# Last layer of a two-layer transformer kernel: rows of a mixture of experts scattered by choice and summed at the end, against rows added into the result by the scatter itself

## What is computed

```python
logits = jnp.clip(xt @ gate_w.T, -50.0, 50.0)       # xt: 2048 tokens x 512, layer-normed; 8 experts
top_w, top_idx = jax.lax.top_k(logits, 2)
rw = jax.nn.softmax(top_w, axis=-1)
# every expert is one 512 x 512 map: W plus a sparse part of its own
out = xt @ W.T + contrib.T                          # = sum over the 2 choices of rw * (map of expert) @ token
x = x + jnp.tanh(g_ffn[1]) * out
```

## Time and profile before

| | us |
|---|---|
| three runs | 2134.19, 2135.01, 2143.93 |
| median | 2135.01 |
| span of the profiled execution, first to last instruction | 2124.4 |
| median over that span (launch and end lie outside the span) | 10.6 |
| last stage, in the span | 1863.6 to 2124.4 |
| its unit loop, first to last scatter | 1960.7 to 2086.0 |
| from the last scatter to the end | 38.4 |

### The profile page before, as it was taken

How to read it: one execution, slowest core, us unless ns; L and a number is a source line. 1 busy time by engine, 2 the same in 40 slices (tenths; PEclk the granted TensorE clock), 3 DMA queues, 4 the chain that set the end, 5 groups by cost and what they waited for, 6 DMA issues and landing times. The chain is left out here.

```text
span 2124.4 us, 39274 instructions
## 1 busy us (share of the span) xinstructions
PE 1848.2 (87%) x11423; PEld 1398.2 (66%) x11423; DVE 1189.7 (56%) x2716; ACT 941.3 (44%) x2679; POOL 996.6 (47%) x1046
## 2 busy tenths in 40 slices
PE   4588999999987999999999999957799998862992
PEld 1355665666556999999999999954466665421781
DVE  5566777777643875422222353328677778670445
ACT  3367676776751432322222333322667666520110
POOL 1477778787621263243333333322655544153551
PEclk9999999999978999999999999988899999985996
DMA  8578877788725588688988888644444454187647
GB/s 321 182 229 275 261 235 232 244 261 252 235 70 183 127 159 191 201 228 259 297 253 239 258 222 220 133 87 123 104 98 109 104 117 101 41 229 207 199 160 272
DMA packets 218788, 409.75 MB, mean 193 GB/s; under 512 B 50794, under 2 KB 116979, under 8 KB 212244
## 3 DMA queue, kind: packets, MB, share of 16 engines
q1 hardware_dynamic: 159132, 319.40, 49.1%
q0 software_dynamic: 31616, 62.14, 13.3%
q10 hardware_dynamic: 27840, 25.70, 4.9%
HBM read 210.46 MB, written 154.20 MB: 172 GB/s over the span
## 5 line engine op out<-in xcount | busy, mean ns | idle before, releaser
L704 ACT ACTIVATE a_P<-a_SC,a_nm 128x256 f32<-128x256 f32 x512 | 235.5, 472 | 132.4 <-DVE a_nm L606 130.8
L1227 POOL DMA_INDIRECT b_y_rows<-b_ysb,b_entry x79 | 124.6, 1577 | 333.8 <-ACT b_ysb L1378 193.6
L606 DVE TENSOR_REDUCE a_nm<-a_SC 128x2 f32<-128x512 f32 x256 | 164.8, 685 | 140.8 <-PE a_SC L850 140.8
L569 POOL TENSOR_TENSOR a_praw<-a_praw,a_phigh 128x704 f32<-128x704 f32 (+2 forms) x126 | 191.5, 1520 | 10.3
L1479 DVE TENSOR_TENSOR b_xl<-b_XT,b_xh 128x512 fp32r<-128x512 f32 x97 | 67.1, 692 | 214.4 <-ACT b_xh L1384 211.7
L861 PEld LDWEIGHTS a_T<-ident,a_P 128*128 128x128 f32 x1024 | 119.2, 145 | 77.8 <-issue 40.4
L861 PE MATMUL a_T<-ident,a_P 128*128 128x128 f32 x1024 | 147.7, 283 | 24.1 <-DVE a_PT L618 22.3
L567 POOL CAST a_phigh<-a_praw 128x704 fp32r<-128x704 f32 (+2 forms) x126 | 111.9, 888 | 95.4 <-DMA a_praw<-in_L_ffn_wd 37.7
L2205 ACT ACTIVATE c_P<-c_SC,c_nm 128x240 f32<-128x240 f32 x256 | 115.5, 456 | 77.1 <-DVE c_P L2077 77.1
L1378 ACT ACTIVATE b_ysb<-b_Y 128x512 f32<-128x512 f32 x79 | 47.2, 597 | 227.2 <-PE b_Y L1322 226.4
L1485 DVE TENSOR_TENSOR b_al<-b_AT,b_ah 128x384 fp32r<-128x384 f32 x111 | 61.9, 558 | 145.9 <-ACT b_ah L1389 145.6
(11 more groups left out here) (519 smaller groups left out, 4984.3 us busy)
## 6 DMA issues: line engine op xcount, KB each, us to landing
w_parts<-a_phigh SPq DMA_DIRECT2D x72, 352.0 KB, 3.7
w_parts<-a_praw SPq DMA_DIRECT2D x72, 352.0 KB, 3.9
b_wh<-w_parts SPq DMA_DIRECT2D x18, 1216.0 KB, 11.7
b_wl<-w_parts SPq DMA_DIRECT2D x18, 1216.0 KB, 14.9
c_q<-c_qT SPq DMA_DIRECT2D x64, 256.0 KB, 4.1
c_k<-c_kT SPq DMA_DIRECT2D x124, 128.0 KB
b_wh<-w_parts SPq DMA_DIRECT2D x18, 704.0 KB, 5.1
b_wl<-w_parts SPq DMA_DIRECT2D x18, 704.0 KB, 7.3
```

The costliest lines, as they stand in the source:

```text
L569: eng.tensor_tensor(raw[:, 0:k * m], raw[:, 0:k * m], r32(high[:, 0:k * m]), ALU.subtract).then_inc(plow_done, 1)
L606: eng.tensor_reduce(nm[:, g % 4, j, :], SC[j][:, :].rearrange("p (t k) -> p t k", t=BT), AX.X, ALU.max, negate=True).then_inc(topped, 1)
L704: e = eng.activation(Pr[:, i, t, :], SC[j][:, t * S:(t + 1) * S], ACT.Exp, bias=nm[:, g % 4, j, t:t + 1], accum_out=den[:, h, t:t + 1])
L1227: eng.indirect_dma_start(out=y_rows, out_offset=bass.IndirectOffsetOnAxis(ap=entry[:, r, 1:2].bitcast(U32), axis=0), in_=ysb[:, v % RING, ...
```

## The change

The result tensor `out` gets 128 rows more (dropped at the end) and first receives the sums x; each unit's rows are then added into it by the scatter.

- `keep_sums` stores x into `out` for batches 0 to 6 during the attention of layer 1 (before: 0 to 3, into a tensor of their own). The last batch and 128 rows of zeros are stored at the head of the last stage.
- A list entry has two values, not three: the place by choice is gone. Empty places point to the 128 rows past the tokens.
- POOL's `send_rows` becomes `add_rows`. A row of `out` is now touched by two units, of different experts. Scatter r waits until scatter r - 2 has landed, and until all scatters of earlier experts have; so the first unit of each expert waits for the unit just before it. Units of the same expert have no token in common, and two of them may be under way. Unit 2 waits for unit 1 too, since the plan's count is at least one scatter, and each of the units 36 to 38 waits for the one before it, since all share the 128 spare rows.
- The plan gets a third row with these counts, by 9 more small operations on VectorE.
- The loads of both choices, the 32 additions, the stores, and the reloads of x are gone.

```diff
-            def send_rows(r):
+            def add_rows(r):
+                if r:
+                    prior = eng.value_load(plan_i[0:1, 2, r:r + 1], min_val=16, max_val=16 * NR)
+                    eng.wait_ge(y_sent[1 - r % 2], prior)
+                    eng.sem_inc(others_added, 1)
+                ge(eng, y_sent[r % 2], 16 * (r // 2))
                 eng.wait_ge(y_scaled, r + 1)
                 eng.indirect_dma_start(
-                    out=y_rows, out_offset=bass.IndirectOffsetOnAxis(ap=entry[:, r, 2:3].bitcast(U32), axis=0),
-                    in_=ysb[:, r % RING, :], in_offset=None).then_inc(y_sent[r % RING], 16)
+                    out=out, out_offset=bass.IndirectOffsetOnAxis(ap=entry[:, r, 1:2].bitcast(U32), axis=0),
+                    in_=ysb[:, r % RING, :], in_offset=None, compute_op=ALU.add).then_inc(y_sent[r % 2], 16)
...
                 if r + AHEAD < NR:
                     gather(r + AHEAD)
+                if r == 0:
+                    eng.wait_ge(sums_stored, 32)
                 if r >= 0:
-                    send_rows(r)
+                    add_rows(r)
...
@@ SP, last stage
             eng.dma_start(raw[:, :], gate_w).then_inc(gw_in, 16)
-            eng.wait_ge(empty_set, 6)
+            eng.dma_start(out[T - S:T, :].rearrange("(t p) d -> p t d", p=P), core.Xa[:, NT - BT:NT, :]).then_inc(sums_stored, 16)
+            eng.wait_ge(zero_set, 1)
+            eng.dma_start(out[T:T + BLOCK, :], zero[:, :]).then_inc(sums_stored, 16)
+            eng.wait_ge(empty_set, 4)
...
-            for i in range(RING):
-                eng.wait_ge(y_sent[i], 16 * ((NR - 1 - i) // RING + 1))
-            for q in range(NG):
-                for k in range(K):
-                    rows = y_rows[k * T + q * GT * P:k * T + (q + 1) * GT * P, :]
-                    eng.dma_start(choice(k, q), rows.rearrange("(t p) d -> p t d", p=P)).then_inc(parts_in[q], 16)
...
+            for q in range(2):
+                eng.wait_ge(y_sent[q], 16 * ((NR + 1 - q) // 2))
@@ VectorE, scaled(r)
-                ge(eng, y_sent[r % RING], 16 * (r // RING))
+                if r >= RING:
+                    eng.wait_ge(y_sent[r % 2], 16 * ((r - RING) // 2 + 1))
@@ SP, attention of layer 1
-                    if n == "O1" and b < B // 2:
+                    if n == "O1" and b < B - 1:
                         keep_sums(b)
```

More of the change, by code:

```diff
@@ L2699, in routed_maps @@
         nb_p, inside, t_e = sb("nb_p", [P, E, E]), sb("inside", [P, 2, E]), sb("t_e", [P, E])
-        plan = sb("plan", [P, 6])
-        plan_i = sb("plan_i", [1, 2, 64], I32)
+        plan = sb("plan", [P, 8])
+        plan_i = sb("plan_i", [1, 3, 64], I32)
         entry = sb("entry", [P, NR, C])
@@ L2725, in routed_maps @@
             sem(n) for n in ("rows_turned", "rows_high", "rows_low", "y_done", "y_scaled")]
-        sums_in = sem("sums_in")
-        y_sent = [sem(f"y_sent{i}") for i in range(RING)]
-        parts_in, out_ready, stored = [sem(f"parts_in{q}") for q in range(NG)], sem("out_ready"), sem("stored")
+        y_sent, others_added = [sem(f"y_sent{i}") for i in range(2)], sem("others_added")
+        zero_set, sums_stored = sem("zero_set"), sem("sums_stored")
         block = ctx.enter_context(nc.Block())
@@ L2781, in _ @@
                 entries(r)
-            for first, n, a in SUMS:
-                eng.dma_start(a, core.x_rows[first * P:(first + n) * P, :].rearrange("(t p) d -> p t d", p=P)
-                              ).then_inc(sums_in, 16)
-            for i in range(RING):
-                eng.wait_ge(y_sent[i], 16 * ((NR - 1 - i) // RING + 1))
-            for q in range(NG):
-                for k in range(K):
-                    rows = y_rows[k * T + q * GT * P:k * T + (q + 1) * GT * P, :]
-                    eng.dma_start(choice(k, q), rows.rearrange("(t p) d -> p t d", p=P)).then_inc(parts_in[q], 16)
[L2791 to L2796, removed]
+            eng.wait_ge(sums_stored, 32)
+            for q in range(2):
+                eng.wait_ge(y_sent[q], 16 * ((NR + 1 - q) // 2))
         @block.gpsimd
         def _(eng):
-            for places, first in ((empty, K * T), (spare, K * T + PADS)):
+            eng.memset(zero[:, :], 0.0).then_inc(zero_set, 1)
+            for places in (empty, spare):
                 eng.memset(places[:, :, 0:1], 0.0).then_inc(empty_set, 1)
-                eng.iota(places[:, :, 1:2].bitcast(I32), pattern=[[1, BLOCK], [0, 1]], base=0,
+                eng.iota(places[:, :, 1:2].bitcast(I32), pattern=[[1, BLOCK], [0, 1]], base=T,
                          channel_multiplier=0).then_inc(empty_set, 1)
-                eng.iota(places[:, :, 2:3].bitcast(I32), pattern=[[1, BLOCK], [0, 1]], base=first,
-                         channel_multiplier=BLOCK).then_inc(empty_set, 1)
             eng.memset(tri[:, :, :], 1.0).then_inc(consts, 1)
@@ L2938, in _ @@
             eng.wait_ge(plan_ready, 1)
-            for i in range(2):
+            for i in range(3):
                 m = eng.transpose(R[0:1, i * 64:(i + 1) * 64], plan[0:64, i:i + 1], core.ident[0:64, 0:64])
@@ L3144, in _ @@
                 scaled(r)
-            eng.wait_ge(sums_in, 16 * len(SUMS))
-            for t in range(NT):
-                added(t)
 def program(nc, x, ctx_1024, fside_BxSx2_0, g_xattn, g_ffn, *args):
```

66 lines of the change are left out of this document (30 added, 36 removed).

## The result

The changed kernel takes 2148.1 us (median of 15 runs, 2142.9 to 2156.3) and the kernel before, in as many runs beside it, 2141.2 (2133.6 to 2146.1). The ratio is 1.0043, with a 95% interval of 1.003 to 1.0057: slower by 0.43%, some 9 us. That is inside the 0.5% band, where the forecast was too, but on the other side of zero, and 2148.1 lies outside the range of 2118 to 2145. Of the 20 us between 2128 and 2148, 6 come from the start (the three runs shown before had a median of 2135.0, all fifteen have 2141.2); the other 14 are the difference itself, +7 by the medians where -7.1 was forecast.

A forecast was written before the change was run, and what follows sets the result against it. TensorE was taken to pace the loop at 3.28 us a unit, before a 38.4 us tail. Tail -38.4, loop +24.1, head +1.5, landing and wake-up +5.7 gave -7.1 us: 2128 us, 8 in 10 within 2118 to 2145.

The forecast's parts named there:

- What goes: End of the kernel: the whole tail of 38.4 us after the last scatter's start goes.
- in its place stands one landing and the wake-up: End of the kernel: the last scatter's landing, 4.8 us, and the wake-up of what waits for it, 0.9 us.
- The loop's sum: Unit loop: twelve serial intervals of 5.66 us, one of 2.5, 25 of 3.16; 149.4 us against 125.3, +24.1.
- Ahead of the loop: Head of the last stage: more bytes stored, fewer of empty entries, +1.5 us; other additions hidden or costed at nothing.
- rival C: Unit loop: gaps on TensorE lower its clock; 10 us if half the spells weren't absorbed, back to 2138, no change; chance 0.07.
- A: Scatters in the loop and at the end land early, after 4.05 to 4.5 us; total below 2124 us; chance 0.27.
- B: Unit loop: DMA engines fill up, landings past 5.46 us make the wait for r - 2 bind everywhere; 2150 us; chance 0.14.
- The sum: Whole kernel: -38.4 + 24.1 + 1.5 + 5.7 = -7.1 us, so 2128 us.

The follow-up runs named there:

- entries12b: The changed kernel with a third, unread column in its list entries, 12 bytes in place of 8; ratio 1.0025 to the kernel before.
- plain_waits: The changed kernel with a plain scatter in place of the accumulating one, all waits kept, the sum left out; 2117.3 us in one run.
- pool_ends_early: The changed kernel without GpSimd's wait for the last two scatters at its end; ratio 1.0037 to the kernel before.
- drains: The changed kernel with three more drains of GpSimd, one ahead of each of the last three scatters; ratio 1.0035 to the kernel before.

## Why the prediction was wrong, by its steps

**"What goes" and "in its place stands one landing and the wake-up": failed, by 8 us.** The landing was right (4.6 against 4.8). The wake-up of 0.9 us was read from waits inside a loop and carried to the end of a stage, where POOL first drains: 9.0 us from landing to the span's end. The drain was a term put at nothing. The drain was in the trace of before, hidden behind the very tail that the change removes. I had asked what hides each added cost, but not what the removed tail was hiding. The runs show it: drained ahead, the end is 6.2 us. (The chain of the earlier trace rows was also read loosely: from 2107.6 to 2118.4 it has 16 of the 32 additions. The 38.4 us don't depend on it.)

**The loop's sum: right in kind, 6.6 us too small.** Twelve serial places, at the units named, 3.17 us for the rest, no catching up: all as written. The twelve took 72.0, 72.7 and 73.2 us, not 67.9. The landings ahead of them had a mean of 5.06 us in the first profile (4.8 to 6.3), and the wake-up was 0.8 to 0.94 but 1.3 to 1.4 at units 10 and 26: 12 x (5.06 + 0.94) = 72.0, if the two are spread over all. The 4.8 was the median of a calm stretch of layer 0, and 5.0 the median here. The other 26 intervals took 84.0, 82.5 and 81.7 against 81.5. In the first profile that is the rest of the 6.6: unit 9 was held 0.5 us by the landing of unit 7 (6.6 us), and 1.8 us came from TensorE, as below under rival C.

**Ahead of the loop: +1.5 was +4 to +8.** I priced the bytes of the stores and credited the smaller entries with fewer bytes. With equal entries (entries12b) the ratio is 1.0025, 5.4 us, about the 6.0 of loop and end; with 8 bytes it is 1.0043. By these ratios, from two chips and with intervals that overlap, the shrunk entry costs 3.9 us, by the heads 7 to 8. The stores themselves show no cost: with 12 bytes the changed kernel's heads were 103.0, 99.3 and 96.3, and those of the kernel before 97.1, 101.9 and 105.8.

**The rivals.** A: it needed landings of 4.5 or less, none was under 4.6. B: landings passed 5.46 for 4 or 5 of 39 scatters in each profile but never as a rule. C: it did come, in small. The granted clock was 0.94 over the loop, with spells at the lower level: four in the first profile, three and two in the others. Here is one of them, ahead of unit 34: TensorE's wait for a gather, the granted clock (third number from the end) in that stretch and the next, and the scatter that was late.

```profile
2110.44 0.66 PE L2888 MATMUL d_XT<-ident,X 128*128 128x128 f32 x4 [1.40 <-DMA X<-b_xn_rows,d_entry]
```

```profile
2111.00:2115.00 4.00, 3.80 (x10) 2.93 (x10) 0.69 (x1) 0.60 (x1) 3.39 (x3) 0.57 0.95 181
2115.00:2121.00 6.00, 6.00 (x31) 4.84 (x30) 2.88 (x4) 1.20 (x2) 3.04 (x4) 1.00 0.82 143
```

```profile
2117.51 1.58 POOL L2819 DMA_INDIRECT out<-d_ysb,d_entry  x1 [0.96 <-DVE d_ysb L3108]
```

The first eight matmuls of that unit took 3.4 us, those of the unit before 2.0. Units 34 and 35 stood 3.83 and 3.27 us behind their forerunners where 3.16 and 2.5 were forecast, and with three intervals of 3.28 after unit 10 TensorE cost 1.8 us in this profile; in the other two unit 35 took 2.59 and 2.29. The gathers were part of it: they landed after 4.3 us in the median and 6.7 at most, where the forecast had 3.4. The drain at the end, the largest single miss, was none of them.

**The sum.** For loop and end I had -8.6 us and the profiles have +6.0; 8.0 of the 14.6 between them is the end with its drain, 6.6 the loop. The fixed cost that the Trainium skill states (page "DMA: Bandwidth & Descriptors", section "Anatomy of one DMA"), added to the scatter's time on the engines, would have made a landing 4.1 us, an estimate; the trace differs, nothing landed under 4.6, and the measurement decides.

Open: why an entry of 8 bytes costs its neighbours more than one of 16. The runs vary only the size, which also shifts the addresses; larger entries weren't tried. The Trainium skill (page "DMA: Bandwidth & Descriptors", section "Specifications") says that below 512 bytes the DMA engines do a read-modify-write; no run here can show it. That holds for all three sizes alike, so it may explain why such writes are dear, but not the order among them that the profiles show. Open too is what fills the drain, counted from the end of the last issue or from its own start, whichever is later: 7.7 us after 39 accumulating scatters, 9.0 after 39 plain ones (`plain_waits` and the kernel before), 7.25 after 36 accumulating ones, but 9.2 for the first of the three added drains.

## What to carry to other kernels

When a change removes the last stretch of a kernel, look on every engine's sequencer for what that stretch was covering; a drain has no row among the busy groups. An ordering wait behind a slow transfer is paid in full if the waiting engine is already at the loop's pace, and nearly not at all if it has slack: with cheap scatters, or with none of the waits, the loop was back at 124 to 127 us. And a smaller record is not a cheaper one: look at the GB/s that its neighbours reach, not at its bytes.

## What the runs showed of the hardware

- A drain of POOL at the end of a stage with 110 indirect DMAs took 7.74 us (39 accumulating scatters) or 9.05 (plain ones, `plain_waits`), the same to the hundredth in the repeats of the changed kernel, and 0.125 us when drains had run shortly before. It can begin while the last transfer is still under way (`pool_ends_early`), and two short ones ended with the landing of the scatter under way (`drains`).
- Beside the same 32 indirect scatters of entries the busy DMA engines moved 159 to 179 GB/s with 8-byte entries, 195 to 260 with 12, 264 to 267 with 16.
- An accumulating scatter of 128 rows of 2 KB takes POOL 1.58 us and lands after 4.6 to 6.6; a plain one 0.98 and 2.7 to 3.8 (`plain_waits`). From a landing to the next dependent scatter's start it is 0.8 to 0.94 us in both, with a few of 1.3 to 1.4 in the changed kernel.
